# Perceiver block on one core: scores and exponentials in pairs of 512 columns, and other steps for the jobs around them

## What is computed

```
xn = layernorm(x, ln_x_g, ln_x_b)            # x here: the context rows
ln = layernorm(latents, ln_l_g, ln_l_b)      # the 64 latents of a batch
q = ln @ Wq
kv = concatenate((xn, ln), axis=1) @ Wkv
k, v = split(kv, 2, axis=-1)                 # 16 heads of 64
sim = einsum("bhid,bhjd->bhij", heads(q) * scale, heads(k))
attn = softmax(where(mask_full, sim, max_neg))
out = einsum("bhij,bhjd->bhid", attn, heads(v))
return layernorm(out.reshape(b, m, INNER) @ Wout, ln_o_g, ln_o_b)
```

## Time and profile before

| | |
|---|---|
| Median of 3 runs | 812.42 us (810.31 to 812.51) |
| Profiled execution, its time | 812.56 us |
| Profiled execution, its span | 810.8 us |
| Mean granted clock of TensorE | 0.978 |
| TensorE, matmul busy | 751.5 us, 93% |
| ScalarE busy | 609.7 us, 75% |
| VectorE busy | 559.9 us, 69% |
| GpSimd busy | 545.3 us, 67% |

### The profile page before, as it was taken

The page is one execution under the profiler, slowest core; times in us unless marked ns, Lnnn a source line. Parts: engine busy times, 40 slices in busy tenths (PEclk is TensorE's granted clock), DMA queues, the critical chain, the costliest instruction groups (busy, mean ns, idle before and its releaser), DMA issues.

```text
span 810.8 us, 22755 instructions
## 1 busy us (share of the span) xinstructions
PE 751.5 (93%) x7122; PEld 418.6 (52%) x7122; DVE 559.9 (69%) x1399; ACT 609.7 (75%) x1086; POOL 545.3 (67%) x745
## 2 busy tenths in 40 slices
PE   5598999999999999999999999999999999899766
PEld 3344544556464555545554655555555546455423
DVE  5776776666666767666666667676766666586677
ACT  5479788887868687888878696868788887865262
POOL 4366676686867768686868677686868686766122
PEclk9799999999999999999999999999999999999797
DMA  5303322121222202121212212121212121110001
GB/s 178 79 6 93 78 75 73 43 61 56 57 60 56 58 17 63 45 71 42 63 52 58 58 55 62 32 58 32 71 45 72 40 60 56 47 43 19 4 1 53
DMA packets 95820, 44.42 MB, mean 55 GB/s; under 512 B 66500, under 2 KB 87848, under 8 KB 95656
## 3 DMA queue, kind: packets, MB, share of 16 engines
q1 hardware_dynamic: 95728, 43.93, 19.5%
q10 hardware_dynamic: 56, 0.05, 0.0%
HBM read 24.20 MB, written 3.34 MB: 34 GB/s over the span
## 4 chain that ended last, share of the span: by engine, by line
PE 65%; DVE 14%; issue 10%; ACT 5%; POOL 3%; DMA 1%; DVEq 1%; ACTq 0%; SPq 0%; POOLq 0%
PE bank L1496 14%; PE bank L1576 7%; PE bank L1459 6%; PE bank L1463 5%; PE bank L1461 5%; PE bank L1414 4%; PE bank L1593 3%; DVE mx L1940 3%; PE bank L1431 3%; PE bank L1611 2%; PE bank L1390 2%; DVE qkl_l L1936 2%; PE bank L1430 2%; PE bank L1648 1%; ACT qkl_h L1118 1%
## 5 line engine op out<-in xcount | busy, mean ns | idle before, releaser
L867 POOL TENSOR_TENSOR p<-arena,p 128x512 f16<-128x512 f32 x256 | 297.9, 1169 | 133.0 <-ACT arena L1137 131.9
L1146 ACT ACTIVATE p<-bank,maskbias 128x512 f16<-128x512 f32 x224 | 155.2, 693 | 103.5 <-PE bank L1463 101.5
L1496 PE MATMUL bank<-p,xv 128*128 128x512 f16 (+1 forms) x768 | 182.3, 380 | 5.3 <-POOL arena L915 3.7
L1940 DVE TENSOR_REDUCE mx<-bank 128x1 f32<-128x464 f32 x256 | 154.0, 632 | 17.8 <-PE bank L1431 16.1
L1137 ACT ACTIVATE arena<-bank,maskbias 128x512 f32<-128x512 f32 x224 | 155.0, 692 | 0.0
L1496 PEld LDWEIGHTS bank<-p,xv 128*128 128x128 f16 (+1 forms) x768 | 58.2, 97 | 74.5 <-issue 25.6
L1936 DVE TENSOR_TENSOR qkl_l<-bank,qkl_h 128x512 f16<-128x512 f32 x64 | 41.1, 686 | 68.9 <-ACT qkl_h L1118 68.8
L1459 PE MATMUL bank<-qkc_h,xtT_h 128*128 128x512 f16 (+1 forms) x256 | 86.5, 389 | 0.0
L1463 PE MATMUL bank<-qkc_h,xtT_l 128*128 128x512 f16 (+1 forms) x256 | 85.0, 379 | 0.0
L1461 PE MATMUL bank<-qkc_l,xtT_h 128*128 128x512 f16 (+1 forms) x256 | 85.0, 379 | 0.0
L1431 PE MATMUL bank<-xtT_h,qkc_h 128*128 128x400 f16 x256 | 83.4, 338 | 0.0
(11 more groups left out here) (283 smaller groups left out, 1576.0 us busy)
## 6 DMA issues: line engine op xcount, KB each, us to landing
arena<-den_dram SPq DMA_DIRECT2D x62, 128.0 KB, 3.2
qkc_h<-arena SPq DMA_DIRECT2D x30, 256.0 KB, 2.4
qkc_l<-arena SPq DMA_DIRECT2D x30, 256.0 KB, 2.5
raw<-in_ctx SPq DMA_DIRECT2D x32, 192.0 KB, 2.4
lt<-lt_dram SPq DMA_DIRECT2D x60, 32.0 KB, 2.1
arena<-in_L_xattn_Wkv SPq DMA_DIRECT2D x1, 1024.0 KB, 7.8
raw<-in_ctx SPq DMA_DIRECT2D x64, 8.0 KB, 2.0
ltT_dram<-x_all SPq DMA_DIRECT2D x4, 256.0 KB, 2.8
```

Of the source, the lines that this page charges most:

```text
L867: g.tensor_tensor(p_halves[0:r, slot, 1, :], p_all[0:r, (plan.halves_made(0, k, t) - 1) % 2, :], p_halves[0:r, slot, 0, :], ALU.subtract). ...
L1146: a.activation(p_halves[0:r, slot, 0, :], sbank[t % SRING][0:r, :], ACT.Exp, bias=bias)
L1496: op = mm(bk[:, :], halves_of[at, row, :], p_halves[at, slot, prob, :], start=tile < 2 and n == 0, stop=last and n == 2)
L1940: v.tensor_reduce(mx[:, hq_tile, part:part + 1], bk[:, 0:width], AX.X, ALU.max).then_inc(s_jobs_taken, 1)
```

## The change

The eight PSUM banks become four pairs of 1024 columns. In plan WINDOW the steps 2 to 7 are wide: at steps 2, 4 and 6 TensorE makes the scores of both halves of a tile, one after the other, and at 3, 5 and 7 none. ScalarE takes each of its two exponentials over both banks in one instruction (`wide_probs`), with p_all as one buffer of 1024 columns, and GpSimd subtracts 1024 columns at once (for the first wide tile in two instructions). The wait for the spread keys comes after the values. The MAX jobs, MT of the even batch, the statistics of the rows, the roots of the odd rows (RSTD) and of x1 (P1), the odd rows' normalisation (XHAT_ODD), and ALIBI, SMAX, SHIFT and EXP get other steps. SyncE loads rows at the top of a pass for the next even batch, and for the odd one in the first half. A wait of move_queries is only written in another way.

```diff
@@ -145,6 +145,10 @@
         made_in = None if isinstance(pair, int) and pair == 0 else pair - 1
         return self.through(made_in, False, kind, None, half)
+    def wide(self, t):
+
+        return self.PAIRED and self.steps[t][1] is not None
+
     def rows(self, t):
         tile, half = self.steps[t]
@@ -169,7 +173,7 @@
...
 WINDOW = Plan(N - 400, ({0, 1, 2, 3, 4}, {0, 1, 2, 3, 4}), dict(
-    STATS={4: (0, 4)}, AGGR=4, RSTD=5, XHAT=6, MASK=5,
+    STATS=[{1: (0, 4)}, {0: (0, 4)}, {4: (0, 4)}], AGGR=[1, 0, 4], RSTD=[5, 2, 5], XHAT=6, MASK=5, XHAT_ODD=5,
     START=dict(QP=[-3, -3], QC=[-2, -2], QL=[-1, -1], T=[-2.5], MAX=[1, 1, 2, 2, 3, 3, 4, 4], MT=4.25),
-    ODD=dict(T=[0], MAX=[2.5, 3, 3, 3.5, 4, 4, 4.5, 5], MT=6), AHEAD=[15.5],
+    ODD=dict(T=[0], MAX=[2.5, 3.5, 4, 4, 4.5, 5, 5.5, 5.5], MT=6), AHEAD=[15.5],
     NEXT=dict(QP=[0, 0.5], QC=[1.5, 6.5], QL=[8.5, 9.5]),
-    EVEN=dict(T=[7.5], MAX=[10.5, 11, 11, 11.5, 12, 12, 12.5, 13], MT=14.25), XV={2: (0, 4)},
-    RDEN=(3, 7), MOVE=11, ST1=[4, 4, 6, 6], YN=[7, 7], XB=8, ST2=8, M0=9, P0=9, X1=10, X1B=20, M1=10, P1=11,
-    XH=12, XHT=13, XHT_OUT=13, QKV=14, QKV_OUT=14, VBLK=15, KEXP=15.5, SC=17, ALIBI=[18, 20], SMAX=21, SHIFT=23, EXP=24,
+    EVEN=dict(T=[7.5], MAX=[10.5, 11.5, 12, 12, 12.5, 13, 13.5, 13.5], MT=14), XV={2: (0, 4)},
+    RDEN=(3, 7), MOVE=11, ST1=[4, 4, 6, 6], YN=[7, 7], XB=8, ST2=8, M0=9, P0=9, X1=10, X1B=20, M1=10, P1=10,
+    XH=12, XHT=13, XHT_OUT=13, QKV=14, QKV_OUT=14, VBLK=15, KEXP=15.5, SC=17, ALIBI=[18, 19], SMAX=20, SHIFT=22, EXP=23,
     PT=[24, 25], PT_OUT=[24, 25], PV=26, CX=27, CXT=28, CXT_OUT=28, WO=29, X2=30, P2=31.5))
@@ -521,7 +525,9 @@
         cxT = sb("cxT", [P, D], F32)
-        bank = [es.enter_context(nc.psum_tensor(f"bank{k}", [P, 512], F32)) for k in range(8)]
+        bank_pairs = [es.enter_context(nc.psum_tensor(f"banks{k}", [P, 1024], F32)) for k in range(4)]
+        bank = [bank_pairs[k // 2][:, 512 * (k % 2):512 * (k % 2) + 512] for k in range(8)]
+        score_pair = bank_pairs[1]
         ubank, sbank, jbank, abank = bank[0:2], bank[2:4], bank[4:6], bank[6:8]
         up_bank = (bank[5], bank[1], bank[0])
...
@@ -745,14 +751,17 @@
                         b, par = i * 2 + k, k
                         pair = i if k == 1 else i - 1
                         more = not (last and k == 1)
+                        if k == 0 and not last:
+                            sp.wait_ge(s_xv_ready, b + 1)
+                            load_ctx(plan, b + 2, 0)
                         if since and k == 0:
                             move_queries(plan, i, 1)
                             rden_spread(b - 2, par)
                         if k == 1 and not last:
                             move_queries(plan, i + 1, 0)
-                        if not last:
+                        if not last and plan is WHOLE and k == 1:
                             sp.wait_ge(s_xv_ready, b + 1)
-                            load_ctx(plan, b + 2, par)
+                            load_ctx(plan, b + 2, 1)
                         if k == 1 and not last:
                             load_queries(plan, i + 2)
...
+                        if k == 0 and not last and plan is WINDOW:
+                            sp.wait_ge(s_xv_ready, b + 2)
+                            load_ctx(plan, b + 3, 1)
...
@@ -861,7 +873,16 @@
             def low_probs(plan, i, k, t):
-                if (k, t) in plan.SPLIT:
+                if plan.wide(t):
+                    if plan.steps[t][1] == 0:
+                        slot = slot_of(plan, k, t)
+                        pool.wait_ge(s_probs_ready, (i * 2 + k) * plan.STEPS + t + 2)
+                        if plan.steps[t][0] == 2:
+                            for half in range(2):
+                                g.tensor_tensor(p_halves[:, slot + half, 1, :], p_all[:, half, :], p_halves[:, slot + half, 0, :], ALU.subtract).then_inc(s_p_lo, 1)
+                        else:
+                            g.tensor_tensor(p_halves[:, slot:slot + 2, 1, :], p_all[:, :, :], p_halves[:, slot:slot + 2, 0, :], ALU.subtract).then_inc(s_p_lo, 2)
+                elif (k, t) in plan.SPLIT:
                     r, slot, made = plan.rows(t), slot_of(plan, k, t), plan.halves_made(i, k, t)
                     pool.wait_ge(s_probs_ready, (i * 2 + k) * plan.STEPS + t + 1)
                     g.tensor_tensor(p_halves[0:r, slot, 1, :], p_all[0:r, (plan.halves_made(0, k, t) - 1) % 2, :], p_halves[0:r, slot, 0, :], ALU.subtract).then_inc(s_p_lo, 1)
@@ -869,7 +890,7 @@
             def ahead(plan, n, par, t):
                 at, CH = plan.at, plan.CH
-                if t == at["RSTD"]:
+                if t == at["RSTD"][2 if isinstance(n, int) and n < 2 else par]:
                     pool.wait_ge(s_ctx_moments, n + 1)
                     g.tensor_tensor(ve[:, 0:CH], mv[:, 0:CH, 1], epsrow[:, 0:CH], ALU.add).then_inc(s_ctx_ve, 1)
...
@@ -1119,13 +1140,32 @@
             def rows_normalised(plan, n, t):
-                if t == plan.at["XHAT"]:
+                if t == plan.at["XHAT" if isinstance(n, int) and n < 2 else "XHAT_ODD"]:
                     act.wait_ge(s_ctx_offset, (n + 1) // 2)
                     for c in range(plan.CH):
                         op = a.activation(raw[:, 1, c, 0:127], raw[:, 1, c, 0:127], ACT.Identity, scale=rstd[:, c:c + 1], bias=offset[:, c:c + 1])
                     op.then_inc(s_xhat_ready, 1)
+            def wide_probs(plan, i, k, t, part):
+
+                gg, slot, chunk = (i * 2 + k) * plan.STEPS + t, slot_of(plan, k, t), plan.chunk(plan.steps[t][0])
+                bias = maskbias[:, k, chunk:chunk + 1]
+                if part == 0:
+                    act.wait_ge(s_scores_ready, gg + 2)
+                    if happened(gg - RING + 2):
+                        act.wait_ge(s_values_done, gg - RING + 2)
+                    a.activation(p_halves[:, slot:slot + 2, 0, :], score_pair[:, :].rearrange("p (a b) -> p a b", a=2), ACT.Exp, bias=bias)
+                else:
+                    made = plan.halves_made(i, k, t)
+                    if happened(made - 1):
+                        act.wait_ge(s_p_lo, made - 1)
+                    a.activation(p_all[:, :, :], score_pair[:, :].rearrange("p (a b) -> p a b", a=2), ACT.Exp, bias=bias).then_inc(s_probs_ready, 2)
+
             def probs(plan, i, k, t, part):
+                if plan.wide(t):
+                    if plan.steps[t][1] == 0:
+                        wide_probs(plan, i, k, t, part)
+                    return
                 b = i * 2 + k
                 gg, tile, r, slot = b * plan.STEPS + t, plan.steps[t][0], plan.rows(t), slot_of(plan, k, t)
                 bias = zrow[0:r, :] if tile == 0 else maskbias[0:r, k, plan.chunk(tile):plan.chunk(tile) + 1]
@@ -1664,14 +1704,19 @@
                     for s in range(2 * plan.STEPS):
                         k, t = divmod(s, plan.STEPS)
                         b = i * 2 + k
-                        scores(plan, i, k, t)
+                        for u in (t, t + 1) if plan.wide(t) else (t,):
+                            if not plan.wide(t) or plan.steps[t][1] == 0:
+                                scores(plan, i, k, u)
                         prep(plan, i, last, s)
-                        background(plan, i, since, s, before_self_scores)
+                        if plan is WHOLE:
+                            background(plan, i, since, s, before_self_scores)
                         if t >= LAG:
                             values(plan, i, k, t - LAG)
                         elif since or k == 1:
                             values(plan, i - 1 + k, 1 - k, t - LAG + plan.STEPS)
                         prep(plan, i, last, s + 0.25)
+                        if plan is WINDOW:
+                            background(plan, i, since, s, before_self_scores)
                         prep(plan, i, last, s + 0.5)
                         background(plan, i, since, s, tail)
                         if since < 2:
@@ -1883,14 +1928,15 @@
             def ahead(plan, n, par, t):
                 at, CH = plan.at, plan.CH
-                if t in at["STATS"]:
-                    if t == min(at["STATS"]):
+                which = 2 if isinstance(n, int) and n < 2 else par
+                if t in at["STATS"][which]:
+                    if t == min(at["STATS"][which]):
                         dve.wait_ge(s_ctx_loaded[par], ctx_count(plan, n, par))
                         if happened(n):
                             dve.wait_ge(s_ctx_rstd, n)
-                    for c in range(*at["STATS"][t]):
+                    for c in range(*at["STATS"][which][t]):
                         v.bn_stats(st[:, c, :], raw[:, par, c, :])
-                if t == at["AGGR"]:
+                if t == at["AGGR"][which]:
                     dve.drain()
                     for c in range(CH):
                         op = v.bn_aggr(mv[:, c, :], st[:, c, :])
```

4 lines of the change are left out of this document (2 added, 2 removed).

## The result

The change makes the kernel slower: 843.3 us (median; 840.61 to 843.85) against 811.37 us (810.08 to 812.51) for the kernel before on the same chip, a ratio of 1.0386 (95% interval 1.0368 to 1.0403). The prediction was 820.2 us, at most 832. The sign was right, the size was not: 32 us over (31.3 between the spans of the two profiled executions), where 8 were forecast.

The account below looks back on a forecast made before the run. TensorE, busy 93% of the span, was taken as the bound. Plus 2.2 minus 1.75 us gave plus 0.45 a pass, 6.3 over fourteen passes; with 1.3 for the ends, 812.6 became 820.2 us, range 806 to 832.

Parts of the forecast that it names:

- rival 4: TensorE's clock falls to 1.2 GHz in the longer stands, giving 862 us; chance 0.02.
- Value block 1, first half: TensorE stands 1.55 us once in each first half, as the block waits for ScalarE's copies behind the wide exponential.
- Value 1 and value 4 of the second half: Second half: block 1 waits some 0.4 us for copies, block 4 0.25 us for the longer GpSimd subtraction.
- What goes: TensorE waits in one pass that the new positions remove, together 1.75 us a pass.
- keys 0.27: Value block 7 no longer waits for the keys GpSimd spreads for self attention: minus 0.28 us a pass.
- statistics 0.31: VectorE's statistics leave the middle of its MAX reductions in the second half: minus 0.37 us a pass.
- odd rows 0.19: Transposes after the last value block wait less, as ScalarE normalises these rows a step earlier: minus 0.20 us.
- QC 0.31 of 0.40: The QC job waits less for VectorE's mT, as SMAX moves a step up: minus 0.40 us a pass.
- TensorE's matmuls stay as they are ... What this costs is order: Matmuls keep number and form, so the wide form's added cost is order only: 2.2 us a pass.
- the signs named for that: Wrong if: pass below 44.1 us, wide exponential under 0.95, score pairs waiting over 0.3 for it, or loop clock under 1.00.
- rival 2: ScalarE or GpSimd run later than counted, so four of six score pairs wait 0.3 us more: 837 us; chance 0.12.
- The ends: First pass, last pass and drain together cost plus 1.3 us, from 0 to 3.

## Why the prediction was right or wrong

- **What bounds the kernel** and the method, one pass start to start: right. The granted clock stayed at 1.00 in the loop, through stands of 1.36 us; rival 4 did not occur. The windows of 44.30 us had been cut at that length, though: by the starts of ST2 ten of the twelve stretches took that, one 45.40 and the last 41.41.
- **Value block 1, first half**: right. 1.55 forecast, 1.36 measured. The wide exponential took 1.02 (1.04 taken); the rest is that it started 0.10 after value 0 for the 0.19 taken, and value 1 0.13 after the copies for 0.22.
- **Value 1 and value 4 of the second half**: plus 0.4 and plus 0.25 forecast, 0.14 and 0.20 measured. The second is as forecast, the first too high.
- **What goes**: 1.75 forecast, 1.63 found: keys 0.27, MAX 0.55 (0.33 and 0.2 forecast), statistics 0.31, odd rows 0.19, QC 0.31 of 0.40 (the block ahead of it is value block 4, where the text says 3). Two small waits that the prediction does not have, at the job QC of step 1 (0.15) and at a MAX job of the second half (0.23), took 0.38 of it back. Taken out of the kernel before by themselves these waits came back elsewhere (812.8 and 819.0 us): they were gains of the arrangement, not of each part.
- **The step that failed** is "TensorE's matmuls stay as they are ... What this costs is order", with the GpSimd subtraction costed as "2.2 at most" and the move of SHIFT and EXP not costed at all. Each duration was taken to hold wherever its instruction is put. The row against it was in the trace: four equal instructions of 127 columns that took 1.94 us where three of them took 0.33 each. Their 1174 ns was an overlap with GpSimd and I had not asked for them, as VectorE was busy 69% and TensorE waited for nothing there. In the change that became 3.97 us and a wait of 1.31 us a pass, some 17 us in all. A pass of 46.1 for 44.6 to 44.9 said that it was wrong, but none of the signs named for that came up: they looked at a faster pass, at ScalarE and at the clock, and this was between VectorE and GpSimd.
- **The score pair exposed everywhere** (rival 2, 837 us) came nearest in time, by another mechanism: pairs wait at most 0.1 us for exponentials.
- **The ends**: plus 1.3 forecast, at most 3; measured 3.9 + 4.7 at the two ends, and 0.5 in the two stretches behind the first ST2 beyond what two of the loop cost, 9.1 in all. Ahead of the first ST2 two value blocks stand 1.27 and 1.52 us where before has 0.39 and 0.94; old positions of MAX and MT with narrow passes there bring it from 106.83 to 105.11, and the rest of the 3.9 was not settled. In the last stretch 2.2 of the 4.7 are the wide form's. Most of the rest goes with P1 at step 10, as the runs with SHIFT back show (28.24, and 25.82 with P1 at 11); in the change itself no run moved P1 alone.

By measured terms a pass of the loop costs 3.39 - 1.63 + 0.05 = 1.81 us more. Fourteen stretches make 22.2 and not 25.3. One stretch of before took 45.40, as TensorE stood 1.12 us there for the DMA that moves mT (L1467; the chain has it at 3.52 us, 2.54 at another place), and the last of them (41.4 before, 41.0 after) has no next pair. With 9.1 at the ends this is, but for rounding, the 31.2.

## What to carry to other kernels

Before costing a move by durations, list the instructions of one form one by one: equal work with unequal time shows an overlap that the move can create or remove, and here it was worth 17 us. A step of one GpSimd instruction, or the form that also sums, removed it at once. Take waits out only together with the arrangement that makes them go: when the waits for the keys and for mT were taken out of this kernel by themselves, the time came back at the next queue. And when cover is put in front of a wait, look at when the block behind it starts: here that did not move (2.32 and 2.33 us after value 0), and the cover waited itself.
